# Two landing buffers for keys and for values, and two for the keys' halves, in a fused attention and expert kernel

## The reference

```python
def reference(x, ctx_1024, gate_w, gate_b, w1, b1, w2, b2):   # x, ctx: (16, 256, 256); w1: (8, 1024, 256)
    def xattn(q, k, v):                     # NHEADS = 16, hd = 16; attention runs over the heads of one token
        qh, kh, vh = q.reshape(B, S, 16, 16), k.reshape(B, S, 16, 16), v.reshape(B, S, 16, 16)
        scores = einsum('bsqd,bskd->bsqk', qh, kh) / 4
        scores = where(tril(ones(16, 16)), scores, -1e18)
        return einsum('bsqk,bskd->bsqd', softmax(scores), vh).reshape(B, S, D)
    def ffn(x):                             # top-1 of 8 experts
        top1 = argmax(x @ gate_w.T + gate_b)
        for e in range(8):
            y = relu(x @ w1[e].T + b1[e]) @ w2[e].T + b2[e]
            out = out + where(top1 == e, y, 0)
    x = x + xattn(layernorm(x), ctx_1024, ctx_1024)
    x = x + ffn(layernorm(x))
```

## Time and profile before

| what | us |
|---|---|
| median of 3 runs | 460.33 |
| lowest, highest run | 457.54, 461.69 |
| the profiled execution | 457.95 |
| its span, first to last instruction | 456.1 |
| TensorE busy | 383.7 (84%) |
| VectorE busy | 336.3 (74%) |
| GpSimd busy | 207.7 (46%) |
| ScalarE busy | 180.6 (40%) |

### The profile page before, as it was taken

The page is one execution under the profiler, slowest core; times in us unless marked ns, Lnnn a source line. Parts: engine busy times, 40 slices in busy tenths (PEclk is TensorE's granted clock), DMA queues, the critical chain, the costliest instruction groups (busy, mean ns, idle before and its releaser), DMA issues.

```text
span 456.1 us, 16303 instructions
## 1 busy us (share of the span) xinstructions
PE 383.7 (84%) x5889; PEld 328.9 (72%) x5889; DVE 336.3 (74%) x777; ACT 180.6 (40%) x317; POOL 207.7 (46%) x213
## 2 busy tenths in 40 slices
PE   0126878996789969995799999988999999999995
PEld 0026767995788968994778887866788888788873
DVE  7779799689892876378657997875677777677773
ACT  2424445454433523243533443333333443433431
POOL 8635544635674558643441354843233333333332
PEclk9999999955555755565589999999899999999999
DMA  7999989978878775678642445678244443444420
GB/s 267 417 273 242 250 206 276 250 197 234 191 182 219 183 164 114 179 154 221 172 119 49 107 97 108 183 156 178 72 115 99 94 100 93 94 108 97 95 63 0
DMA packets 125802, 73.17 MB, mean 160 GB/s; under 512 B 99229, under 2 KB 110238, under 8 KB 125216
## 3 DMA queue, kind: packets, MB, share of 16 engines
q1 hardware_dynamic: 96336, 60.46, 51.5%
q0 software_dynamic: 3408, 8.46, 5.0%
q10 hardware_dynamic: 25984, 3.21, 4.9%
HBM read 48.28 MB, written 11.24 MB: 130 GB/s over the span
## 4 chain that ended last, share of the span: by engine, by line
PE 52%; DMA 9%; POOL 9%; SPq 9%; DVE 9%; issue 9%; ACT 2%; POOLq 0%; ACTq 0%; DVEq 0%
PE s_ps L1510 19%; PE at_ps L1526 6%; PE pv_ps L1526 6%; PE s_ps L1406 4%; POOL sorted_rows L1343 4%; PE pv_ps L1436 4%; DMA arena<-qv_hl 4%; PE at_ps L1527 3%; PE pv_ps L1527 3%; PE lg_ps L1463 3%; PE tr_ps L1448 2%; DMA v_in<-v_t 2%; SPq L603 2%; DVE arena L1189 2%; DMA sorted_rows<-pay,slot_i 2%
## 5 line engine op out<-in xcount | busy, mean ns | idle before, releaser
L1510 PEld LDWEIGHTS s_ps<-arena 128*128 x1872 | 133.1, 99 | 43.4 <-issue 5.1
L1510 PE MATMUL s_ps<-arena 128*128 128x128 f16 x1872 | 157.7, 222 | 2.5 <-DMA arena<-arena 2.5
L1206 DVE SCALAR_TENSOR_TENSOR arena<-arena,s_ps 128x512 f32<-128x512 f32 x78 | 53.4, 685 | 30.4 <-PE s_ps L1510 29.6
L1369 POOL DMA_INDIRECT result<-arena x39 | 38.8, 995 | 64.6 <-DVE arena L1231 54.9
L1406 PEld LDWEIGHTS s_ps<-k_hl,arena 128*128 128x128 f16 x1536 | 54.4, 118 | 18.0 <-DMA arena<-qv_hl 13.1
L1436 PE MATMUL pv_ps<-a_hl,arena 128*128 128x16 f16 x1536 | 53.6, 178 | 15.4 <-DMA arena<-qv_hl 12.5
L1436 PEld LDWEIGHTS pv_ps<-a_hl,arena 128*128 128x128 f16 x1536 | 52.8, 118 | 18.4 <-DMA arena<-qv_hl 15.0
L1406 PE MATMUL s_ps<-k_hl,arena 128*128 128x16 f16 x1536 | 54.1, 178 | 12.5 <-DMA arena<-qv_hl 12.2
L1362 POOL TENSOR_TENSOR arena<-arena 128x256 f32<-128x256 f32 x39 | 29.9, 766 | 74.3 <-DMA arena<-b 69.4
L1526 PE MATMUL at_ps<-arena,k_in 128*128 x160 | 61.3, 385 | 2.1 <-DVE k_hl L1217 2.0
L1526 PE MATMUL pv_ps<-arena,x_in 128*128 x152 | 57.6, 379 | 1.1 <-DVE x_in L1217 1.1
(11 more groups left out here) (141 smaller groups left out, 580.3 us busy)
## 6 DMA issues: line engine op xcount, KB each, us to landing
arena<-w SPq DMA_DIRECT2D x28, 512.0 KB, 5.9
arena<-sorted_rows SPq DMA_DIRECT2D x39, 130.0 KB, 2.5
arena<-b SPq DMA_DIRECT2D x39, 128.0 KB, 3.2
arena<-qv_hl SPq DMA_DIRECT2D x70, 64.0 KB, 3.4
k_in<-k_t SPq DMA_DIRECT2D x16, 256.0 KB, 3.6
arena<-x SPq DMA_DIRECT2D x4, 1024.0 KB, 10.3
x_in<-x_t SPq DMA_DIRECT2D x16, 256.0 KB, 5.0
v_in<-v_t SPq DMA_DIRECT2D x16, 256.0 KB
```

Source lines behind the costliest of these rows:

```text
L1206: eng.scalar_tensor_tensor(out=h_in[:, c].rearrange("p (k t) -> p k t", t=P), in0=bias, scalar=W_SCALE, in1=h_ps[c][:].rearrange("p (k t) ...
L1369: eng.indirect_dma_start(out=out, out_offset=bass.IndirectOffsetOnAxis(ap=rows[:, r, :].bitcast(I32)[:, D + 2:D + 3], axis=0), in_=rows[:, ...
L1510: k = eng.matmul(o, weights_of(j, w + k_ * H + n * P, P), xt[:, j % XB, a + k_], start=(k_, w, a) == (0, HI_1, 0), stop=k_ == KD - 1 and w ...
```

## The change

`k_in`, `v_in` and `k_hl` get a second copy, and chunk `i` uses copy `i % 2`. Each landing buffer has a semaphore of its own. The loads of keys `i` and of values `i` now wait for the low halves of chunk `i - 2` (the count `i - 1`), and ACT's cast of keys `i` for the scores of chunk `i - 2`. `v_hl` stays single, and so does the wait before the cast of values. In the experts' part the first copy takes the place of the single buffer. No number of the order tables changes: each engine has the same instructions in the same order.

```diff
--- before.py
+++ after.py
@@ -420,9 +420,9 @@
         x_in = sb("x_in", [P, 2, CW])
         qv_hl = sb("qv_hl", [P, 3, BLK // 2, HEADS, 2, 2], F16)
         q_hl, v_hl = (qv_hl[:, 2], qv_hl[:, 0]), qv_hl[:, 1]
-        k_in = sb("k_in", [P, CW])
-        k_hl = sb("k_hl", [P, BLK, 2, HEADS], F16)
-        v_in = sb("v_in", [P, CW])
+        k_in = sb("k_in", [P, 2, CW])
+        k_hl = sb("k_hl", [P, 2, BLK, 2, HEADS], F16)
+        v_in = sb("v_in", [P, 2, CW])
         a_sb = sb("a_sb", [P, CW])
         spread = a_sb[:, 0:2 * P].rearrange("p (s u b) -> p s u b", s=2, b=G)
         a_hl = sb("a_hl", [P, BLK, 2, HEADS], F16)
@@ -482,8 +482,8 @@
         h_in = v_flat[:, 0:4 * HALF].bitcast(F32).rearrange("p (n c) -> p n c", n=2)
         b1_cols = carve(q_flat, 4 * KH).bitcast(F32).rearrange("p (n k) -> p n k", n=2)
         b2_rows = carve(q_flat, 4 * D).bitcast(F32).rearrange("p (n c) -> p n c", n=2)
-        h_hi = [z.bitcast(F16) for z in (k_in[:], x_in[:, 0, :])]
-        h_lo = [k_hl[:].rearrange("p n a q -> p (n a q)"), x_in[:, 1, :].bitcast(F16)]
+        h_hi = [z.bitcast(F16) for z in (k_in[:, 0], x_in[:, 0, :])]
+        h_lo = [k_hl[:, 0].rearrange("p n a q -> p (n a q)"), x_in[:, 1, :].bitcast(F16)]
 
         s0_bank, s1_bank, at_bank, pv0_bank, pv1_bank, st_bank, tr_bank, lg_bank = [ps(n) for n in
             ("s0_ps", "s1_ps", "at_ps", "pv0_ps", "pv1_ps", "st_ps", "tr_ps", "lg_ps")]
@@ -507,7 +507,7 @@
         s_own = [sem(f"s_own{n}") for n in range(2)]
         s_wide = [sem(f"s_wide{n}") for n in range(4)]
         s_xs = [sem(f"s_xs{n}") for n in range(NG)]
-        s_kin, s_vin = [sem(n) for n in ("s_kin", "s_vin")]
+        s_kin, s_vin = [[sem(f"{w}{n}") for n in range(2)] for w in ("s_kin", "s_vin")]
         s_bd = [sem(f"s_bd{n}") for n in range(2)]
         s_xr = [sem(f"s_xr{n}") for n in range(CG)]
         s_gate, s_fill = [sem(n) for n in ("s_gate", "s_fill")]
@@ -558,7 +558,7 @@
         def values_landed(i):
             return s_bd[i % 2], 128 * (i // 2 + 2)
 
-        last_home = v_in[:], a_sb[:]
+        last_home = v_in[:, 0], a_sb[:]
 
         def chunk_of(n):
             e, c = n // PER_EXPERT, n % PER_EXPERT
@@ -634,14 +634,14 @@
             def load_k():
                 for i in range(NC):
                     yield
-                    sp.wait_ge(s_k_lo, i)
-                    eng.dma_start(k_in[:], kt_v[i]).then_inc(s_kin, 16)
+                    sp.wait_ge(s_k_lo, i - 1)
+                    eng.dma_start(k_in[:, i % 2], kt_v[i]).then_inc(s_kin[i % 2], 16)
 
             def load_v():
                 for i in range(NC):
                     yield
-                    sp.wait_ge(s_v_lo, i)
-                    eng.dma_start(v_in[:], vt_v[i]).then_inc(s_vin, 16)
+                    sp.wait_ge(s_v_lo, i - 1)
+                    eng.dma_start(v_in[:, i % 2], vt_v[i]).then_inc(s_vin[i % 2], 16)
 
             def load_residual():
                 for i in range(NC):
@@ -791,17 +791,17 @@
             def keys():
                 for i in range(NC):
                     yield
-                    act.wait_ge(s_kin, 16 * (i + 1))
-                    act.wait_ge(s_qk, i)
-                    eng.copy(k_hl[:, :, 0, :], k_in[:].rearrange("p (n k) -> p n k", k=HEADS)).then_inc(s_k_hi, 1)
+                    act.wait_ge(s_kin[i % 2], 16 * (i // 2 + 1))
+                    act.wait_ge(s_qk, i - 1)
+                    eng.copy(k_hl[:, i % 2, :, 0, :], k_in[:, i % 2].rearrange("p (n k) -> p n k", k=HEADS)).then_inc(s_k_hi, 1)
 
             def values():
                 for i in range(NC):
                     yield
-                    act.wait_ge(s_vin, 16 * (i + 1))
+                    act.wait_ge(s_vin[i % 2], 16 * (i // 2 + 1))
                     if i >= 1:
                         act.wait_ge(*values_landed(i - 1))
-                    eng.copy(halves(v_hl, 0), v_in[:].rearrange("p (b d u) -> p b d u", u=2, d=HD)).then_inc(s_v_hi, 1)
+                    eng.copy(halves(v_hl, 0), v_in[:, i % 2].rearrange("p (b d u) -> p b d u", u=2, d=HD)).then_inc(s_v_hi, 1)
 
             def spread_first_queries():
                 for i in range(2):
@@ -1289,14 +1289,14 @@
                 for i in range(NC):
                     yield
                     pool.wait_ge(s_k_hi, i + 1)
-                    eng.tensor_tensor(k_hl[:, :, 1, :], k_in[:].rearrange("p (n k) -> p n k", k=HEADS),
-                                      k_hl[:, :, 0, :], ALU.subtract).then_inc(s_k_lo, 1)
+                    eng.tensor_tensor(k_hl[:, i % 2, :, 1, :], k_in[:, i % 2].rearrange("p (n k) -> p n k", k=HEADS),
+                                      k_hl[:, i % 2, :, 0, :], ALU.subtract).then_inc(s_k_lo, 1)
 
             def values():
                 for i in range(NC):
                     yield
                     pool.wait_ge(s_v_hi, i + 1)
-                    eng.tensor_tensor(halves(v_hl, 1), v_in[:].rearrange("p (b d u) -> p b d u", u=2, d=HD),
+                    eng.tensor_tensor(halves(v_hl, 1), v_in[:, i % 2].rearrange("p (b d u) -> p b d u", u=2, d=HD),
                                       halves(v_hl, 0), ALU.subtract).then_inc(s_v_lo, 1)
 
             def weights_of_softmax():
@@ -1403,7 +1403,7 @@
                     pe.wait_ge(s_k_lo, i + 1)
                     for n in range(BLK):
                         for q, k in ((0, 0), (0, 1), (1, 0)):
-                            m = eng.matmul(s[:, n], q_bd[i % 2][:, n // 2, :, n % 2, q], k_hl[:, n, k, :],
+                            m = eng.matmul(s[:, n], q_bd[i % 2][:, n // 2, :, n % 2, q], k_hl[:, i % 2, n, k, :],
                                            start=False, stop=(n, q) == (BLK - 1, 1))
                     m.then_inc(s_qk, 1)
```

## The result

| | before | with the change |
|---|---|---|
| median of 20 runs, us | 459.16 | 461.73 |
| lowest, highest | 456.69, 461.69 | 458.91, 467.66 |
| profiled execution: time, span | 457.95, 456.1 | 461.60, 459.8 |

The ratio is 1.006, 95% interval 1.0038 to 1.0081. So the change costs about 2.6 us, small but clear of no change. The forecast was 460.4 with a range of 456.5 to 463.5 and 0.78 for within 1%; all three came out as said. The sum behind it did not: it had +0.1. All ratios leave out, for each kernel, the runs over 1.5% above its own fastest, which can take 7 of 29 runs from one kernel and none of 12 from the other, so the medians of all runs stand beside a ratio where they say something else. Here they give 1.006 too.

A forecast was written before the change was run, and what follows sets the result against it. The prediction saw the changed first part as a web of waits with no engine full. Cast of keys -0.5 and stretched DVE +0.6 gave +0.1 us: 457.95 to 458.1, for the median 460.4, range 456.5 to 463.5.

The forecast's parts named there:

- Loads, gain zero: SP's queue: 15 loads each of keys and values may issue earlier, but nobody waited for them, so 0 us.
- ACT's cast of keys 13: At 171.61: cast 1.5 us earlier, low half of values 12 0.47 us earlier, passed on as -0.5 us.
- DVE stretched by 0.6 us: Near 109.55: POOL's halves back to back delay one L1189 by 1.2 us, a later one gains 0.6; net +0.6.
- Transfers in each other's way: Earlier loads among spread transfers: three places, 0 to 1.6 us each, taken as 0.
- rival D: Loads delay landings at three places, 1.6 us each: +4.8 us, 465.1, slower by 1.0%; chance 0.05.
- L: Theory made after the result: the load of keys itself, sooner in the queue, is in the way.
- Rival A: All ACT's waits for scores ahead of casts of keys pass through: 6.2 us gained, 454.1, faster by 1.3%; chance 0.09.
- Rival B: SP's queue: two spreads go 0.80 us sooner, no DVE operation is stretched: -2.1 us, 458.2; chance 0.13.
- Rival C: POOL's four moved low halves each stretch an L1189 by 1.64 us: +6.6 us, 466.9, slower by 1.4%; chance 0.05.
- Rival E: Nothing moves at all, since queues keep their order and the next instruction waits anyway: 460.3; chance 0.05.
- R: Theory made after the result: what the wait had held back behind the load of keys is in the way once released.

The follow-up runs named there:

- both holds: Early keys alone, and the whole change, each with SP waiting behind every load of keys for the old low half; 1.0014 and 1.0018 against the kernel before.
- old waits: The change's second copies and semaphores kept, all three waits put back as before, against the kernel before: 1.0017.
- the quarter loads' control: The kernel before, with each load of keys cut to a quarter of its columns from chunk 2 on, against the kernel before: 1.0011.
- their quarter loads: Only loads of keys early, each cut to a quarter of its columns from chunk 2 on, against the kernel before: 1.0034.
- both changed orders: Kernel before, single buffers, loads of keys moved behind loads of weights, queries or residuals at six places (1.0072) or five (1.0052).

## Why the forecast held and its sum did not

Part of it is luck. The forecast started from 460.33, the median of the first 3 runs; over 20 runs the same kernel has 459.16. The sum was off by 2.5 us (+0.1 against +2.6), the time by 1.3.

**Loads, gain zero: right.** 42.8 us of waits on SP went and nobody was faster for it. The waits had cost nothing, since apart from the very start no engine waited for these landings.

**ACT's cast of keys 13: right up to its last step.** ACT and then POOL with the change, the view of the earlier trace rows:

```profile
171.01 2.44 ACTq L603 DMA_DIRECT2D arena<-qv_hl  x2
173.50 0.62 ACT L796 CAST k_hl<-k_in 128x512 f16<-128x512 f32 x1 [1.90 <-issue]
174.02 0.78 ACT L788 CAST qv_hl<-x_in 128x512 f16<-128x512 f32 x1
176.04 0.64 ACT L851 ACTIVATE a_sb<-a_sb 128x512 f32<-128x512 f32 x1 [1.24 <-DVE a_sb L995]
176.58 0.81 ACT L804 CAST qv_hl<-v_in 128x512 f16<-128x512 f32 x1
```

```profile
174.20 1.16 POOL L1292 TENSOR_TENSOR k_hl<-k_in,k_hl 128x512 f16<-128x512 f32 x1 [2.76 <-ACT k_hl L796]
...
177.47 1.30 POOL L1299 TENSOR_TENSOR qv_hl<-v_in,qv_hl 128x512 f16<-128x512 f32 x1 [0.71 <-ACT qv_hl L804]
```

The cast starts 0.05 us after ACT's spread transfers, as said, and the low half of values 12 starts 0.08 us behind its cast (176.58 + 0.81 = 177.39), where it had been 0.5 us. Against the rest of the program the place stands 3.0 us later at the exponentials and 2.6 at the low half, which is the 0.4 to 0.5 us of the forecast. The next step, "From there POOL is busy with scatters up to the spread at 191.53, so I let it pass on", is the one that fails. DVE and then POOL just behind, first in the kernel before and then with the change:

```profile
174.85 0.15 DVE L1097 CAST slot_i<-lg_ps 128x8 int32<-128x8 f32 x1
174.96 1.18 DVE L1123 TENSOR_TENSOR ready<-full,done 1x8 f32<-1x8 int32 x1
...
176.29 1.07 POOL L1343 DMA_INDIRECT sorted_rows<-pay,slot_i  x1 [0.16 <-issue]
```

```profile
177.82 0.96 DVE L1119 TENSOR_SCALAR full<-count_c 1x8 int32<-1x8 int32 x1
178.71 0.15 DVE L1097 CAST slot_i<-lg_ps 128x8 int32<-128x8 f32 x1
...
179.66 1.07 POOL L1343 DMA_INDIRECT sorted_rows<-pay,slot_i  x1 [0.90 <-DVE slot_i L1097]
```

POOL's next scatter needs `slot_i`, which DVE makes. In both kernels one of DVE's tiny operations lasts until POOL has made its low half. Before, that was L1123, behind `slot_i` (1.18 us, to 176.14; POOL's low half ends at 176.13). With the low half 0.4 us sooner it is L1119, ahead of `slot_i` (0.96 us where it had 0.15, to 178.78; POOL's ends at 178.77). So the scatter stands 0.3 us further behind the exponentials than before (3.62 us against 3.28), and the gain is gone at once. All four kernels with an early cast have this wait of 0.90 us, and none of the other ten. The two runs with only the cast early give -0.1% and -0.2%, the right sign, not clear of zero, and not from this place.

**DVE stretched by 0.6 us: wrong.** POOL and DVE at the place of the earlier trace rows, with the change:

```profile
111.52 1.30 POOL L1285 TENSOR_TENSOR qv_hl<-x_in,qv_hl 128x512 f16<-128x512 f32 x1 [3.07 <-ACT qv_hl L788]
112.76 1.60 POOL L1292 TENSOR_TENSOR k_hl<-k_in,k_hl 128x512 f16<-128x512 f32 x1
```

```profile
111.58 1.78 DVE L1189 SCALAR_TENSOR_TENSOR arena<-arena 128x512 f16<-128x512 f32 x1
...
114.48 0.68 DVE L1189 SCALAR_TENSOR_TENSOR arena<-arena 128x512 f16<-128x512 f32 x1
```

POOL's halves do stand back to back, as said. But DVE's operation still took 1.78 us, not 2.9: it got in between the two, and POOL's second took 1.60 us in place of 1.16. The later L1189, 1.25 us before, took 0.68. So these two operations took 0.6 us less together, where I had charged 0.6.

**Transfers in each other's way, taken as zero: by all that the runs say, this is the step that failed.** The loss, 2.6 us, has the sign and about half the size of rival D (4.8), and the early loads of keys bring it by themselves (1.0065) while the early cast does not (0.9988). The reason I gave, that a load behind SP's spreads overtakes nothing, looked at loads of keys and values alone. I had counted in the order rows which waits go, and not what else stood behind each wait. The wait for keys also held back loads of queries, weights and residuals, some for 3 to 5 us. By their points both holds give most of the loss back (1.0014, 1.0018), which speaks for these followers. Letting them past with single buffers gave 1.0052, but that run is no proof, as said there. L as a part is not excluded by the intervals, nor is a share of the values of up to 0.4%.

**Rival A** (6.2 us gained) falls with the two runs of the cast alone. **Rival B's** premise, ACT's share of the spread on the chain, was not tested by itself. **Rival C** (6.6 us lost) is out by the run with only the cast early, at most 1.0013, and its first place by the DVE rows above. **Rival E** is out by SP's waits.

**What stays open** is the last link: by which transfer's delay the released loads cost. I looked for later landings of the spread transfers. PE's wait for them ahead of the outputs, from the changed kernel and then from the one with only the cast early:

```profile
  DMA arena<-qv_hl: 33.1, 16
```

```profile
  DMA arena<-qv_hl: 34.0, 14
```

It is as long in the kernel that lost nothing as in the one that lost. Another landing does tell them apart. POOL's scatters (L1343) write a group's rows from `pay`, which exists once, so ACT's copy of the next group's rows (L844), on which TensorE's transposes wait, stands until the last scatter has landed. The chain of waits goes through this landing, before and with the change:

```profile
137.97 4.12 DMA sorted_rows<-pay,slot_i
```

```profile
139.24 5.82 DMA sorted_rows<-pay,slot_i
```

It took 4.1 to 4.6 us in the six profiles in which neither the loads of values nor, at this place, those of keys or weights go past a wait: before, old waits, cast alone, halves alone, early keys to chunk 7, and the quarter loads' control. With the hold behind the load of keys it took 4.73 and 4.95 us, and 5.0 to 6.1 in the five kernels in which a load of weights goes past the wait there (the change, the early keys, their quarter loads, both changed orders). Only early values, with 5.3 us, do not fit R. So one late transfer that somebody waits for was none of SP's but POOL's: 1.7 us more on the chain in the profile of the change. That the loads beside it delay it was not tested by itself, and each figure is from one execution.

One profile of each kernel cannot carry 2.6 us, since single executions of one kernel differ by as much. The runs show which edit costs. Why it does is argued from the holds and from this landing, and not shown. The granted clock does not order the kernels: its mean over the runs is 0.848 with only the cast early, which lost nothing, and 0.852 with the followers first at six places, which lost.

## What to carry to other kernels

A wait in a transfer queue also paces everything queued behind it. Before taking one away, list the rows behind it up to the next transfer that somebody waits for, with their bytes, and ask what they will run beside, transfers of other engines' queues too. If nobody waits for the landing that a second buffer would bring sooner, keep the wait. If a buffer is to be doubled, take the one whose reader holds up an engine. That was here the keys' halves, and doubling them alone gave no loss and no gain clear of zero. And a gain on one engine is passed on only as far as what the engine does next needs nothing from another.

## What the runs showed that was not expected

A DVE operation that waits for POOL can be let in between two POOL operations that stand back to back: 1.78 us for DVE and 1.60 in place of 1.16 us for POOL's second. In another place of the kernel before it waited out both and took 2.32 us. Which of the two happens was not settled.

The 96 score matmuls of a chunk are sometimes split by idle time that ends with nothing the profile shows. With the change, PE at 131 us:

```profile
131.24 3.14 PE L1406 MATMUL s_ps<-k_hl,arena 128*128 128x16 f16 x89 [2.21 <-issue]
```

The kernel with only the halves doubled has such a gap of 1.40 us at the same group and is not slower, and the kernel with only the keys early, which lost as much as the change, has none over 0.47 us. So it does not explain the loss.
